# Silu for both gates of the mixer on ScalarE, two steps moved to GpSimd, and a new order of every queue

## What is computed

```python
xz = x @ in_proj_w.T;  x_in, z = xz[..., :D], xz[..., D:]
x_conv = silu(causal_conv(x_in) + conv_b)
p = x_conv @ x_proj_w.T;  B, C = p[..., :N], p[..., N:2*N]
dt = softplus(p[..., -1:] * dt_proj_w + dt_proj_b)
h_t = exp(dt * -exp(A_log)) * h_(t-1) + dt * B * x_conv
y_t = sum_n(h_t * C)
out = (y * silu(z)) @ out_proj_w.T
```

```python
log_A = clip(cumsum(log(a)), -80);  h = exp(log_A) * cumsum(b * exp(-log_A))
```

## Time and profile before

| | us |
|---|---|
| median of 3 runs (lowest, highest) | 961.77 (959.21, 962.63) |
| profiled execution | 961.2 |
| its span, first to last instruction | 959.4 |

### The profile page before, as it was taken

One profiled execution on the slowest core, in us unless ns is written; L12 is line 12 of the kernel. 1 busy time (PEld: TensorE's weight loads), 2 busy tenths in 40 slices (PEclk: granted clock), 3 DMA queues, 4 the chain that ended last, 5 costly groups with the idle time before them and its releaser, 6 DMA issues. The chain is left out here.

```text
span 959.4 us, 9608 instructions
## 1 busy us (share of the span) xinstructions
PE 796.9 (83%) x2802; PEld 528.2 (55%) x2802; DVE 802.2 (84%) x1013; ACT 671.6 (70%) x1345; POOL 561.4 (59%) x468
## 2 busy tenths in 40 slices
PE   2385867978987799999899999998998797787585
PEld 1264644736554556475647564756476546546464
DVE  5245566677799999999999999999999999989761
ACT  4347687588767865997699769876976685465452
POOL 0202457437836793789378937893776376565421
PEclk9597977989998889999999999999999799789597
DMA  9000000000100010001000100010000000000000
GB/s 315 12 23 22 23 1 22 1 1 0 56 1 0 1 42 13 0 1 59 8 1 1 60 1 0 1 46 0 1 1 27 1 1 1 23 0 1 22 1 22
DMA packets 10341, 19.49 MB, mean 20 GB/s; under 512 B 1457, under 2 KB 5297, under 8 KB 10289
## 3 DMA queue, kind: packets, MB, share of 16 engines
q1 hardware_dynamic: 10288, 18.88, 5.8%
HBM read 14.69 MB, written 4.19 MB: 20 GB/s over the span
## 5 line engine op out<-in xcount | busy, mean ns | idle before, releaser
L385 POOL TENSOR_TENSOR y<-y,hC 128x1024 f32<-128x1024 f32 (+3 forms) x140 | 280.1, 2001 | 77.3 <-DVE hC L1461 73.4
L1914 PE MATMUL pC<-w,hT 128*128 128x256 f32 x1024 | 232.4, 382 | 4.9 <-ACT hT L754 4.9
L819 ACT ACTIVATE dA<-dt,A_neg 128x512 f32<-128x512 f32 (+3 forms) x320 | 187.5, 630 | 54.3 <-DVE hs L1450 53.8
L1914 PEld LDWEIGHTS pC<-w,hT 128*128 128x128 f32 x1024 | 194.5, 191 | 36.7 <-issue 7.2
L1450 DVE TENSOR_TENSOR_SCAN hs<-dA,carry,pS 128x512 f32<-128x512 f32 (+3 forms) x192 | 193.4, 1008 | 18.1 <-ACT dA L819 10.4
L2037 PE MATMUL pS<-stack,sel 97*128 97x512 f32 (+3 forms) x320 | 148.0, 515 | 54.5 <-DVE hs L1450 54.0
L1435 DVE TENSOR_TENSOR pS<-u,pS 128x1024 f32<-128x1024 f32 (+3 forms) x160 | 159.8, 999 | 17.4 <-PE pS L2037 16.8
L1461 DVE TENSOR_TENSOR hC<-hs,pS 128x1024 f32<-128x1024 f32 (+3 forms) x160 | 157.5, 985 | 15.3 <-PE pS L2037 15.1
L1450 DVE TENSOR_TENSOR_SCAN hs<-dA,pS 128x512 f32<-128x512 f32 (+1 forms) x128 | 138.2, 1080 | 14.6 <-POOL carry L392 6.0
L754 ACT ACTIVATE hT<-pA,ffb_sb 128x512 f32<-128x512 f32 (+3 forms) x160 | 94.7, 599 | 59.2 <-PE pA L1907 58.9
L1907 PE MATMUL pA<-tg,w 128*128 128x512 f32 (+3 forms) x320 | 127.9, 538 | 7.7 <-ACT hT L754 6.3
(11 more groups left out here) (120 smaller groups left out, 1101.5 us busy)
## 6 DMA issues: line engine op xcount, KB each, us to landing
xt<-xT SPq DMA_DIRECT2D x6, 515.0 KB, 4.7
xtok<-x SPq DMA_DIRECT2D x6, 512.0 KB, 5.3
out<-x3b SPq DMA_DIRECT2D x6, 512.0 KB, 2.9
w<-w1a SPq DMA_DIRECT2D x1, 1024.0 KB, 8.3
w<-w2a SPq DMA_DIRECT2D x1, 1024.0 KB, 10.4
w<-w1b SPq DMA_DIRECT2D x1, 1024.0 KB, 8.3
w<-w2b SPq DMA_DIRECT2D x1, 1024.0 KB, 9.9
xt<-xT SPq DMA_DIRECT2D x2, 259.0 KB, 7.8
```

Of the source, the lines that this page charges most:

```text
L385: nc.gpsimd.tensor_tensor(y[:, :, 0:ch.T], so_far, hC[:, n % CRING, :, 0:ch.T], ALU.add).then_inc(S["y_sum"], 1)
L819: nc.scalar.activation(dA[:, k % ARING, 0:ch.T], dt[ch.side][:, h, 0:ch.T], ACT.Exp, scale=A_neg[:, h, n:n + 1]).then_inc(S["dA_ready"], 1)
L1914: mm = nc.tensor.matmul(dst[:, b * D:b * D + D], src(k, t0), w[:, k, :], start=k == 0, stop=k == nk - 1)
```

## The change

Both gates are computed as Silu by ScalarE alone; the four tanh and (tanh + 1) * x steps are gone with their semaphores, and so are the factors 0.5 behind them. `decay_steps` and `readout` are done by GpSimd, as the same arithmetic. The first `z_silu` of a chunk waits for the readout of the chunk before the last, since the buffer `zz` has two sides. The order of all four engines' queues is new in all four kinds of step; SyncE's is not. No tile, split or matmul changes.

```diff
+            def decay_steps(ch):
+                c = ch.i
+                pool.wait_ge(S["la_scan"], 2 * c + 2)
+                nc.gpsimd.tensor_tensor(decay[:, :, 0:ch.T], st[:, 0:H, 1:1 + ch.T], st[:, 0:H, 0:ch.T], ALU.subtract).then_inc(S["dl_ready"], 1)
+
+            def readout(ch, gate):
+                if gate is not None:
+                    conv_done(pool, gate)
+                pool.wait_ge(S["y_sum"], ADDS * (ch.i + 1))
+                nc.gpsimd.tensor_tensor(yg[:, :, 0:ch.T], y[:, :, 0:ch.T], zz[ch.side][:, :, 0:ch.T], ALU.mult).then_inc(S["yg_ready"], 1)
...
-            def z_tanh(ch, h):
+            def z_silu(ch, h):
+                if ch.i > 1:
+                    act.wait_ge(S["yg_ready"], ch.i - 1)
                 act.wait_ge(S["z_mm"], H * ch.i + h + 1)
-                nc.scalar.activation(zz[ch.side][:, h, 0:ch.T], pC[h][:, 0:ch.T], ACT.Tanh, scale=0.5).then_inc(S["tz_ready"], 1)
+                nc.scalar.activation(zz[ch.side][:, h, 0:ch.T], pC[h][:, 0:ch.T], ACT.Silu).then_inc(S["zz_ready"], 1)
...
-                nc.scalar.activation(v[:, :, 0:ch.T], cv[:, :, 0:ch.T], ACT.Tanh, scale=0.5).then_inc(S["tcv_ready"], 1)
+                nc.scalar.activation(v[:, :, 0:ch.T], cv[:, :, 0:ch.T], ACT.Silu).then_inc(S["v_ready"], 1)
...
-                V.scalar_tensor_tensor(out=u[:, :, 0:ch.T], in0=dt[ch.side][:, :, 0:ch.T], scalar=0.5, in1=v[:, :, 0:ch.T], op0=ALU.mult,
-                                       op1=ALU.mult).then_inc(S["u_ready"], 1)
+                V.tensor_tensor(u[:, :, 0:ch.T], dt[ch.side][:, :, 0:ch.T], v[:, :, 0:ch.T], ALU.mult).then_inc(S["u_ready"], 1)
```

More of the change, by code:

```diff
@@ L397, in opening @@
                 if gate is not None:
+                    decay_steps(gate)
                     inv_rms(gate)
@@ L426, in entry @@
                     sum_states(tail, NS - 1)
+                    readout(tail, gate)
                 if prep is not None:
@@ L477, in entry @@
                 if scan is not None:
+                    save_carry(scan, 13)
+                if gate is not None:
+                    add_bias(LN_GATE, 0, x1, x1b, S["x1b_ready"], gate)
+                if scan is not None:
+                    save_carry(scan, 14)
+                    sum_states(scan, 13)
+                if ahead is not None:
+                    conv_add(ahead, 2)
+                if tail is not None:
+                    row_scales(LN_OUT, tail)
+                if ahead is not None:
+                    conv_add(ahead, 3)
@@ L494, in entry, with closing @@
                     save_carry(scan, 15)
-                if ahead is not None:
-                    conv_add(ahead, 3)
-            def step(ahead, gate, prep, scan, tail):
+            def closing(ahead, gate, prep, scan, tail):
                 if scan is not None:
@@ L876, in opening @@
                     relu(0, gate, 5)
-                if ahead is not None:
-                    conv_tap(ahead, 2, prep)
+                if prep is not None:
+                    state_decay(prep, 4)
                 if gate is not None:
@@ L956, in entry @@
                     relu(1, tail, 3)
+                if scan is not None:
+                    state_decay(scan, 10)
+                if gate is not None:
+                    over_rms(gate)
+                if tail is not None:
                     relu(1, tail, 4)
                 if prep is not None:
-                    mconv_tap(prep, 3)
-                if scan is not None:
-                    state_decay(scan, 8)
-                if gate is not None:
-                    squares(gate)
-                if prep is not None:
-                    mconv_tanh(prep)
+                    mconv_silu(prep)
                 if tail is not None:
@@ L1020, in step @@
             def step(ahead, gate, prep, scan, tail):
+                if scan is not None:
+                    state_decay(scan, 0)
+                    state_decay(scan, 1)
                 if tail is not None:
@@ L1223, in closing @@
                     state_decay(scan, 14)
-                if prep is not None:
-                    step_sizes(prep)
-                if scan is not None:
                     state_decay(scan, 15)
@@ L1548, in entry @@
                         state_scan(scan, 0, 1)
-                if tail is not None:
-                    readout(tail, gate)
+                        state_input(scan, 1)
+                        state_scan(scan, 1, 0)
                 if prep is not None:
@@ L1612, in entry @@
                     state_scan(scan, 8, 0)
-                if prep is not None:
-                    mconv_silu(prep)
-                if scan is not None:
                     state_output(scan, 7)
@@ L1651, in entry @@
                     state_input(scan, 15)
-                if prep is not None:
-                    dt_x(prep)
-                if scan is not None:
                     state_scan(scan, 15, 0)
@@ L1703, in step @@
                     state_input(scan, 4)
-                if gate is not None:
-                    decay_steps(gate)
-                if scan is not None:
                     state_scan(scan, 4, 0)
                     state_output(scan, 3)
+                if gate is not None:
+                    log_A(gate)
+                    a2_minus_1(gate)
+                if scan is not None:
                     state_scan(scan, 4, 1)
@@ L1799, in closing @@
                     state_input(scan, 1)
-                if prep is not None:
-                    add_ffn0(prep, 0, tail)
-                if scan is not None:
                     state_scan(scan, 1, 0)
@@ L1837, in closing @@
                     state_scan(scan, 7, 1)
-                if prep is not None:
-                    z_silu(prep, 0)
-                if scan is not None:
                     state_input(scan, 8)
@@ L2132, in entry @@
                     down(0, prep, 1, 1)
+                if gate is not None:
+                    gate_mm(gate, 0, 0)
+                    gate_mm(gate, 0, 1)
+                if tail is not None:
+                    out_proj1(tail, prep)
                 if scan is not None:
@@ L2235, in entry @@
                     spread_B(prep, 0)
+                if gate is not None:
+                    down(0, gate, 0, 0, tail=tail)
                 if scan is not None:
```

863 lines of the change are left out of this document (408 added, 455 removed).

## The result

The changed kernel takes 974.4 us (median of 4 runs, 972.7 to 978.5) against 961.4 us; the ratio is 1.0142, 95% interval 1.0109 to 1.0174. Its profiled execution has a span of 971.6 us, against 959.4.

A forecast was written before the change was run, and what follows sets the result against it. VectorE was taken as the bound from 275 to 831 us, with a closed loop across the engines taking over in the full steps; 961.2 + 9 - 3 + 1 + 1 = 969 us, range 962 to 978.

The forecast's parts named there:

- The loads: ScalarE: Silu alone in its table, 77 loads for 40 in the steps, eight per full step, 1.4 us each.
- the rival that shared Exp's table: Silu sits in Exp's table, so no load more and a loop of 93.9 us: 944 us, chance 0.04.
- Full steps: Three steps, 373 to 659 us: a closed loop of waits takes over as the bound, +3 us each, +9.
- The loop's pieces: One feed-forward residual add (`add_ffn0`) to the next: 1.5 + 43.8 + 17.8 + 16.1 + 18.9 = 98.1 us, before 95.04.
- the rival in which gains and losses cancel: The loop is 96 us instead of 98, or the order doesn't do what it says: 957 to 966, chance 0.13.
- VectorE's saving: Decay step, readout and gate passes leave VectorE: 4.6 us less per full step, 1.1 us comes back, 3.5 saved.
- a pair: VectorE: an input product right before the scan that reads it costs 0.27 us extra; 11 per full step instead of 7.
- Before 275: The filling steps: nine more loads, 12.6 us, most in waits, gates lose a VectorE pass; +1, bounds -4 and +9.
- 275 to 373 and after 659: Steps beside the full ones: loop shorter than VectorE's sum, so its saving counts; -1 us in each of three, -3.
- the end: Four more loads beside short scans with slack, last readouts on the slower engine: +1, bounds -2 and +3.
- The rival with the loads everywhere: Loads delay exponentials with a lead of two states, so steps outside the full ones also lose: 980, up to 992; chance 0.13.
- Signs foretold: 80 loads, loop some 98 us, VectorE under 95% busy with idle before `add_ffn0` and state 10's scans, GpSimd near 79%.

The follow-up runs named there:

- the tanh build: The changed kernel with Tanh in place of both Silu calls, every queue order kept: 972.4 us, ratio 1.0111, 43 table loads.
- the build that lost 29 us: The changed kernel with row squares, first gate products and clip of the full step put back to earlier places: 1003.1 us; with tanh 1001.5 us.
- the build with the mixed readout: The kernel before, tanh and old order, with decay step of chunks 0 to 4 and readout of chunks 0 and 1 on GpSimd: 957.5 us.

## Why the prediction was right, and where it was not

The forecast was 969 us, slower; measured 974.4, in the range and of the likeliest sign. That is in part luck: the sum hides two errors that partly cancel, 5.6 us too much in the full steps and 11.2 too little before them.

**The loads: count and price right.** 80, eight per full step, 1.28 us each, and Silu alone in its table: the rival that shared Exp's table was wrong.

**Full steps: +9 forecast, +3.4 measured.** The loop's pieces came out near: to the eighth relu 43.2 (43.8), to the first up 17.0 (17.8), ups 15.6 (16.1), `down(0, ...)` to the add 18.4 (18.9). Each forecast was over by half to eight tenths of a microsecond, which is 2.4 us a loop for this one and 1.1 and 1.3 for the two ahead of it. At 96 to 97 us the loop is in the place of the rival in which gains and losses cancel; the total left that rival's range for another reason, the fill. The gate products between the halves of `down(0, ...)` made the loop's last piece longer, as said. But the agreement of the first piece is partly luck. I took three loads for +4.2 on it; the tanh build puts them at +0.9, since in the new order this piece also waits for GpSimd. The waits inside it, which I carried over from the old order, were in truth others.

**VectorE's saving: 3.5 us a step forecast, 2.0 measured** ((281.00 - 275.11) / 3). The second figure is busy time alone, and of the 0.27 us that I put on a pair 0.20 is idle, so the like forecast is 4.6 - 4 x 0.07 = 4.3; the pairs came out as counted, four more in a step (36 for 24 in the three). The sentence at fault is the one that found no row of the steady steps with a VectorE operation held by GpSimd and left it there. The new order made such rows: 6.5 us in three steps, about 2.2 a step. It is the order far more than the move: with tanh, both steps on GpSimd and the old order this product takes 1.23 us on average in the launch (the product ahead of it, L1391, is held there instead, 1.53 us for 1.23), in the changed kernel 2.18. In return GpSimd's sums of states for 512 tokens became shorter, 2421 ns for 2487 on 84 of them, 5.5 us in a launch (3.0 us over sums of all sizes). So the change didn't take the two engines' reads apart; it moved some of the collisions to the busier engine. The new products, and every old one at a new time, had to be walked against each VectorE operation with two SBUF inputs. The holders are not the moved products alone; the one shown is an old one at a new time. Whether the full steps would be faster without the holding was not tried. The Trainium skill ("SBUF — State Buffer") describes an exclusive lock of the port pair that the two engines share, for a whole instruction, and names VectorE operations with two inputs in SBUF, not any two inputs as I wrote; the line at 506.40 us agrees with it.

**Before 275: +1 forecast, +12.2 measured.** This is the step that failed, above its bound of +9. It counted loads (12.6 us) and gate passes and took "most in waits". That was right: with tanh this stretch ends only 1.4 us earlier. What it left out was the order itself. I walked the queues of the full step and not those of the opening and the entry, where a state takes VectorE 2.8 us and a block of ups 7 to 8, so that the place of a spread counts. VectorE waits 9.8 us more for spreads there. Putting the fill's order back took 8.4 us off the start of chunk 2, 4.4 off that of chunk 3 and 5 off the total; where the rest of the 12.2 us comes from stays open.

**275 to 373 and after 659: -3 forecast, -1.4 and -3.1 measured; the end +1 forecast, +1.1 measured.** There VectorE's saving counts, as argued. The idle time of ScalarE's late decays was smaller than my walk had it: VectorE's waits for decays over chunks 6 to 8 are 2.3 us, as many as before.

**The rival with the loads everywhere** names a mechanism that is real, in another order: 992 us with the old one, there without the GpSimd steps. It wasn't the state decays with their lead of two, as I had it, but `root_exp`, for which VectorE waits with no lead at all. What guards the changed kernel, as I read the traces, is that both `z_silu` stand behind `root_exp`; no run moved these two calls alone. The long wait ahead of the row squares, which I held to be the other danger, is there with the loads and without them, and VectorE's longest waits in the build that lost 29 us come from a spread behind the gate products.

**Signs foretold.** VectorE at 95% in the full steps (under 95 forecast), GpSimd at 76% (79), busy sum of VectorE -22 us (-40). Idle time before `add_ffn0` is nearly absent there (0.4 us in three steps), and before scans ended by decays 1.7 us: as I read it, the loop and VectorE run neck and neck, where I had the loop alone as the bound.

## What to carry to other kernels

A fixed cost such as a table load has no price of its own in an in-order queue: 37 more loads cost 2 us where they fill waits, 39 more cost 31 us where one stands before a result that a full engine wants next. Price a new order in every kind of step, the filling ones too: here most of the loss arose there, where the tiles of the state loop are short beside the blocks of matmuls. When work moves to an engine that shares a path to memory, look for instructions of unchanged shape that became longer; the saving may be paid back there.

## What the chip showed that I had not expected

- A VectorE product with both inputs in SBUF was held until a GpSimd product, begun shortly before it, had ended, and then took its usual length: 3.38 us for 1.22 when GpSimd's 2.36 us product had begun 0.07 us earlier. Mean over six in the launch 2.18 us; the summing scan is held too (up to 3.31 for 1.25). It goes the other way as well, as the earlier trace rows had it.
- Every load of a table took 1.283 us, whichever function it was for, and the next activation began 0.01 to 0.02 us behind it.
- The granted clock moved a little without a change on TensorE itself: 0.95 against 0.90 in chunk 2, on the same matmuls, in the build with the mixed readout. Both figures are means over the stretch. The cause is open.
